# Spreading the inverted softmax denominators over the partitions by DMA instead of by a TensorE product

## What is computed

```
x = x + tanh(g_xattn[0]) * L0_xattn(layernorm(x), ctx, ctx)
x = x + tanh(g_ffn[0]) * L0_ffn(layernorm(x))
x = x + tanh(g_xattn[1]) * L1_xattn(layernorm(x), ctx, ctx)
x = x + tanh(g_ffn[1]) * L1_ffn(layernorm(x))
```

```
scores = jnp.einsum('bhqd,bhkd->bhqk', qh, kh) / jnp.sqrt(jnp.float32(d_k))
attn = jax.nn.softmax(scores, axis=-1)
context = jnp.einsum('bhqk,bhkd->bhqd', attn, vh)
return context.transpose(0, 2, 1, 3).reshape(B, S, H * dk) @ w_out + b_out
```

## Time and profile before

| | |
|---|---|
| device time, median of 3 runs | 1260.38 us (1259.9 to 1260.52) |
| span of the profiled execution | 1044.2 us |
| median less span (start and end of a launch) | 216.2 us |
| TensorE busy | 927.7 us, 89% of the span |
| VectorE busy | 624.5 us, 60% |
| ScalarE busy | 581.2 us, 56% |
| GpSimd busy | 679.4 us, 65% |
| chain that ended last | PE 57%, DVE 13%, ACT 9%, DMA 7%, issue 7%, POOL 6% |

### The profile page before, as it was taken

The page is one execution under the profiler, slowest core; times in us unless marked ns, Lnnn a source line. Parts: engine busy times, 40 slices in busy tenths (PEclk is TensorE's granted clock), DMA queues, the critical chain, the costliest instruction groups (busy, mean ns, idle before and its releaser), DMA issues.

```text
span 1044.2 us, 25012 instructions
## 1 busy us (share of the span) xinstructions
PE 927.7 (89%) x8892; PEld 777.6 (74%) x8892; DVE 624.5 (60%) x1600; ACT 581.2 (56%) x1274; POOL 679.4 (65%) x905
## 2 busy tenths in 40 slices
PE   5999988788748999999999989887998999999992
PEld 3777776566647989999999977775776767778881
DVE  5899999988964563244625759784735424533320
ACT  2888876687525446544644667554555455444540
POOL 6565556578747777377427777621686758878785
PEclk9999998899868999999999999998999999999997
DMA  9355432122145656676566663123164554574444
GB/s 367 117 177 183 153 123 100 38 67 68 52 157 161 209 176 205 201 213 188 163 193 187 195 236 103 43 71 90 17 114 49 91 68 50 81 105 54 51 54 45
DMA packets 130811, 130.87 MB, mean 125 GB/s; under 512 B 33410, under 2 KB 103426, under 8 KB 129794
## 3 DMA queue, kind: packets, MB, share of 16 engines
q1 hardware_dynamic: 100466, 91.82, 27.8%
q0 software_dynamic: 28928, 29.91, 17.5%
q10 hardware_dynamic: 1296, 7.54, 1.8%
HBM read 54.01 MB, written 49.62 MB: 99 GB/s over the span
## 4 chain that ended last, share of the span: by engine, by line
PE 57%; DVE 13%; ACT 9%; DMA 7%; issue 7%; POOL 6%; ACTq 0%; SPq 0%; POOLq 0%; DVEq 0%
PE psum L844 10%; PE psum L854 10%; PE psum L1022 9%; PE psum L1012 8%; PE psum L656 3%; ACT w_sb L1669 3%; PE psum L976 2%; POOL work L1970 2%; DVE mx L1156 2%; DVE w_sb L1162 2%; ACT work L1676 1%; PE psum L834 1%; DMA out_x<-ln_sb,dest 1%; PE psum L683 1%; DMA odd<-ln_sb,dest 1%
## 5 line engine op out<-in xcount | busy, mean ns | idle before, releaser
L1763 ACT ACTIVATE hid_sb<-psum,work 128x128 f32<-128x128 f32 (+1 forms) x424 | 145.6, 412 | 138.9 <-PE psum L844 136.6
L1970 POOL DMA_INDIRECT work<-yg,place x128 | 122.7, 959 | 73.6 <-issue 48.2
L844 PE MATMUL psum<-work 128*128 128x128 f32 (+1 forms) x848 | 150.1, 320 | 2.6 <-issue 2.3
L854 PE MATMUL psum<-w_sb,hid_sb 128*128 x1192 | 150.2, 275 | 0.0
L854 PEld LDWEIGHTS psum<-w_sb,hid_sb 128*128 128x128 f32 x1192 | 144.8, 192 | 2.1
L1012 PE MATMUL psum<-work,w_sb 128*128 128x272 f32 (+2 forms) x512 | 131.0, 397 | 5.1 <-ACT ctx_sb L1872 3.1
L2044 POOL DMA_INDIRECT out_x<-ln_sb,dest x68 | 106.2, 1562 | 45.0 <-DVE ln_sb L1586 24.8
L844 PEld LDWEIGHTS psum<-work 128*128 128x128 f32 x848 | 124.4, 192 | 11.3 <-issue 4.2
L1872 ACT ACTIVATE ctx_sb<-psum,w_sb 128x272 f32<-128x272 f32 (+2 forms) x256 | 115.8, 488 | 26.3 <-PE psum L1012 22.5
L1022 PE MATMUL psum<-ctx_sb,w_sb 128*128 128x272 f32 (+2 forms) x512 | 128.1, 392 | 0.0
L2044 POOL DMA_INDIRECT odd<-ln_sb,dest x68 | 105.5, 1552 | 32.3 <-issue 16.1
(11 more groups left out here) (241 smaller groups left out, 1762.3 us busy)
## 6 DMA issues: line engine op xcount, KB each, us to landing
work<-w_sb SPq DMA_DIRECT2D x76, 322.0 KB
work<-xg SPq DMA_DIRECT2D x73, 128.0 KB
yg<-yg_sb SPq DMA_DIRECT2D x73, 128.0 KB
xg<-yg_sb SPq DMA_DIRECT2D x24, 384.0 KB, 4.1
ctx_sb<-tok SPq DMA_DIRECT2D x8, 1088.0 KB, 6.4
ctxn<-sums_sb SPq DMA_DIRECT2D x64, 64.0 KB, 2.0
out_x<-x_sb SPq DMA_DIRECT2D x16, 256.0 KB
odd<-yg_sb SPq DMA_DIRECT2D x10, 384.0 KB, 2.9
```

The costliest lines, as they stand in the source:

```text
L844: e.matmul(banks[UP_BANKS[c]][:, 0:cols], w1g(b)[:, c * P:c * P + P], xgT_sb[:, u % 2, at:at + cols], start=True, stop=True).then_inc(s_up, 1)
L854: ins = e.matmul(banks[DOWN_BANKS[b % 2]][:, n * D:n * D + D], hid0[:, b % 2, c, n * P:n * P + P], w2_sb[:, bass.ds(number, 1), c, :].rear ...
L1763: e.activation(hid0[:, b % 2, c, 0:cols], banks[UP_BANKS[c]][:, 0:cols], ACT.Gelu, bias=w1g(b)[:, HID + c:HID + c + 1]).then_inc(s_hg, 1)
L1970: e.indirect_dma_start(dst[:, k, :], None, yg_dram[h], at).then_inc(s_get[i], 16)
```

## The change

The table, its load and TensorE's product are gone. In their place SyncE waits for the reciprocal and issues two SBUF-to-SBUF DMAs per pair into `rb_sb`, a part of `work`; each writes 128 partitions of 128 columns, reading every one of 16 rows of `den_sb` eight times. The normalisation reads `rb_sb` in place of PSUM. The denominators are brought by two DMAs of 16 partitions (in another order of rows) in place of four of 8. VectorE's reciprocal now stands ahead of stats0 in its iteration. TensorE's wait for the copied sums moves from the table's product to the output product, where it comes later. SyncE waits for the last normalisation before its loop over the expert blocks, since a weight buffer there overlays `rb_sb`.

```diff
+        rb_sb = cut(10240, dict(i=2, n=2 * P), "i n")
...
-                w.wait_ge(s_dc[i], 64 * (p // 2))
+                w.wait_ge(s_rb[i], 32 * (p // 2))
                 w.wait_ge(s_vc[i], 32 * (p // 2))
                 for a in range(2):
-                    for u in range(2):
-                        row, at = 8 * (2 * a + u), 2 * P * a + P * u
-                        e.dma_start(den_sb[row:row + 8, i, :], sums_sb[ONES:P:HEAD_ONES - ONES, i, at:at + P]).then_inc(s_dc[i], 16)
+                    e.dma_start(den_sb[16 * a:16 * a + 16, i, :], sums_sb[ONES:P:HEAD_ONES - ONES, i, 2 * P * a:2 * P * a + 2 * P]
+                                ).then_inc(s_dc[i], 16)
...
+            def spread_rden(p):
+                i = p % 2
+                w.wait_ge(s_rden, p + 1)
+                w.wait_ge(s_cn, p - 1)
+                for u in range(2):
+                    e.dma_start(rb_sb[:, i, u * P:u * P + P],
+                                den_sb[u:32:2, i, :].unsqueeze(1).to_broadcast([2 * DH, DH, P])).then_inc(s_rb[i], 16)
...
                 for _ in range(2):
                     next(filling, None)
+                spread_rden(p)
...
+            w.wait_ge(s_cn, NP)
             for b in range(NBL + 2):
...
-            def spread_rden(p):
-                w.wait_ge(s_rden, p + 1)
-                w.wait_ge(s_uc, min(p + 2, NP))
-                w.wait_ge(ld["tables"], 112)
-                for u in range(2):
-                    ins = e.matmul(banks[B_C][:, u * P:u * P + P], spread_sb[0:32, u, :], den_sb[0:32, p % 2, :], start=True, stop=True)
-                ins.then_inc(s_sp, 1)
-
             def output(p):
                 w.wait_ge(s_cn, p + 1)
+                w.wait_ge(s_uc, min(p + 2, NP))
...
-                if 0 <= p - 3 < NP:
-                    spread_rden(p - 3)
...
             def normalise(p):
                 i = p % 2
-                w.wait_ge(s_sp, p + 1)
+                w.wait_ge(s_rb[i], 32 * (p // 2 + 1))
                 w.wait_ge(s_vc[i], 32 * (p // 2 + 1))
-                e.tensor_tensor(ctxn[:, i, :], banks[B_C][:, 0:2 * P], ctxn[:, i, :], ALU.mult).then_inc(s_cn, 1)
+                e.tensor_tensor(ctxn[:, i, :], rb_sb[:, i, :], ctxn[:, i, :], ALU.mult).then_inc(s_cn, 1)
...
-                stats0(20 + 2 * p, 2)
                 if 0 <= p - 2 < NP:
                     invert(p - 2)
+                stats0(20 + 2 * p, 2)
```

More of the change, by code:

```diff
@@ L372, in build @@
             "s_v", "s_vx", "s_st0", "s_st1", "s_sc", "s_mx", "s_sub", "s_exp", "s_rden", "s_xb", "s_uc")]
-        s_pt, s_pT, s_av, s_sp, s_cn, s_o, s_x1 = [sem(n) for n in ("s_pt", "s_pT", "s_av", "s_sp", "s_cn", "s_o", "s_x1")]
-        s_dc, s_vc = [[sem(f"{n}{i}") for i in range(2)] for n in ("s_dc", "s_vc")]
+        s_pt, s_pT, s_av, s_cn, s_o, s_x1 = [sem(n) for n in ("s_pt", "s_pT", "s_av", "s_cn", "s_o", "s_x1")]
+        s_dc, s_vc, s_rb = [[sem(f"{n}{i}") for i in range(2)] for n in ("s_dc", "s_vc", "s_rb")]
         s_xT0, s_xl, s_xe, s_xlt, s_lgx, s_lg = [sem(n) for n in ("s_xT0", "s_xl", "s_xe", "s_xlt", "s_lgx", "s_lg")]
@@ L451, in sync_program @@
             for dst, src in ((small_sb, "small"), (mask_sb, "mask"), (before_sb, "before"), (block_sb, "block"), (b2T_sb, "b2T"),
-                             (rowcol_sb, "rowcol"), (spread_sb, "spread")):
+                             (rowcol_sb, "rowcol")):
                 load("tables", dst[:], t_in[src])
@@ L772, in count0 @@
                 w.wait_ge(s_ch, h + 1)
-                w.wait_ge(ld["tables"], 112)
+                w.wait_ge(ld["tables"], 96)
                 wait_bank(B_P)
@@ L1166, in invert @@
                 i = p % 2
-                w.wait_ge(s_dc[i], 64 * (p // 2 + 1))
+                w.wait_ge(s_dc[i], 32 * (p // 2 + 1))
                 e.reciprocal(den_sb[0:32, i, :], den_sb[0:32, i, :]).then_inc(s_rden, 1)
@@ L1680, in copy_sums @@
                 w.wait_ge(s_av, p + 1)
-                w.wait_ge(s_dc[i], 64 * (p // 2))
+                w.wait_ge(s_dc[i], 32 * (p // 2))
                 w.wait_ge(s_vc[i], 32 * (p // 2))
@@ L2085, in lay_out @@
     order = np.arange(D).reshape(4, 2, 2 * DH).transpose(1, 0, 2).reshape(-1)
-    spread = np.zeros((P, 2, P), np.float32)
-    for n, (pa, u, m, h) in enumerate(itertools.product(range(2), range(2), range(4), range(2))):
-        at = 64 * pa + 16 * m + DH * h
-        spread[n, u, at:at + DH] = 1.0
     w = [a["L0_xattn_w_q"], a["L0_xattn_w_k"], a["L0_xattn_w_v"], a["L0_xattn_w_out"][order], a["L1_xattn_Wq"], a["L1_xattn_Wk"],
@@ L2121, in lay_out @@
         "rowcol": f((r % NS)[:, None] + NS * np.arange(NT // NS)[None, :], r[:, None]),
-        "spread": spread,
         "before": c(np.stack([(q < k), np.ones((P, P))], 1).astype(np.float32)),
```

3 lines of the change are left out of this document (removed).

## The result

| | kernel before | changed |
|---|---|---|
| median, lowest to highest, 17 runs each, us | 1259.89, 1251.88 to 1264.28 | 1266.29, 1261.4 to 1273.89 |
| profiled execution, us | span 1044.2, no time of its own | time 1267.35, span 1265.5 |
| large maximum of iterations 3 and 17, us | 39.60, 144.49 | 39.87, 155.20 |
| one iteration between them, us | 7.49 | 8.24 |

The change makes the kernel slower, by about 0.6%: ratio 1.0057, with a 95% interval of 1.0039 to 1.0076. The forecast was 1256.0 us, 0.3% faster. Only runs in the fast state are compared; single runs, whose state is unknown, are used for their profiles alone.

A forecast was written before the change was run, and what follows sets the result against it. Attention was bound by a loop through ScalarE and TensorE, VectorE's 6.88 us next; -8.6 + 5.4 + 2.2 - 2.2 - 1.2 = -4.4 us from 1260.38 gave 1256.0 us, own range 1252 to 1258.5, overall 1250 to 1264.

The forecast's parts named there:

- What bounds the kernel: Layer 0's attention: table's product costs 1.30 us a turn; without it VectorE's 6.88 us bounds, TensorE at 6.2.
- The step that failed: Spread's landing before the normalisation: 2.65 us from the reciprocal, taken from the channels' DMA, 0.4 us to spare.
- 3.03 us of cover: Time from the reciprocal's end until VectorE alone could start the normalisation: 3.03 us.
- The -8.6 us: Gain in iterations 3 to 17: 14 turns, each 0.61 us shorter, from 7.49 to 6.88.
- The landing of 2.0 to 2.3: Sign expected in the changed profile: the spread lands 2.0 to 2.3 us after issue.
- The queue: First 19 iterations: bursts of fills, turned inputs and weights delay the spread; +5.4 us, ends 0 and about 9.
- Fills alone are over before the spread's data come: Within the queue term: iterations with only zero fills were to cause no stall.
- GpSimd's port, +2.2: Normalisation reading two SBUF tiles: +0.1 us for each of 14 plus about 8 later ones, +2.2 us.
- rival B: GpSimd holds back VectorE's normalisations, 0.4 us for each of 22: +4.2, total 1260.2 us; chance 0.15.
- Later waits and the tail, -3.4: Waits on table's and output products: -2.2 us behind iteration 17, -1.2 us at the end.
- Rival C: Attention: DMAs' latency closes a new loop, 3.85 us plus latency, break-even 3.64; 1265 us, slower; chance 0.18.
- The baseline: Profiled span of 1044.2 us against runs' median of 1260.38: 216.2 us difference, left as it was.

The follow-up runs named there:

- experiment 5: Changed kernel with normalisation, output product, residual and router's statistics one iteration later: 1041.67 us, 0.9984 of the kernel before; turn 6.86 us.
- experiment 2: Changed kernel with all 38 zero fills issued before the first pair: 1270.29 us, turn 7.59 us against 8.24 in the changed kernel.
- experiment 12: Changed kernel, fills first, spread reading 128 different partitions, beside a partner with the repeated source: turn 7.51 against 7.69 us; an earlier probe was inconclusive.
- experiment 3: Changed kernel with the spread issued right behind the sums, ahead of turned inputs, weights and fills: ratio 1.0040, turn 8.32 us.
- experiment 6: Changed kernel with all zero fills first and VectorE's reciprocal ahead of the residual: turn 7.77 us.
- experiment 10: Version of experiment 5 with a catch-up at the end: 1247.73 us, ratio 0.9936 on the first chip; 1044.50 us, ratio 1.0000 on the second.
- experiment 1: Kernel before, unedited, profiled again: 1255.41 us, ratio 0.9994, turn 7.49 us.

## Why the prediction was wrong

**What bounds the kernel: right.** The copy of the sums and the product did leave the chain, and VectorE is the next bound: 6.70 us in an undisturbed iteration of experiment 5, where I had added up 6.88. TensorE I had too low: 6.2 us a turn, where it is busy 6.65 in experiment 5.

**The step that failed** is "the landing of the second ... I take 2.65, since 2.0 is the median of 64: in a quiet queue 0.4 us to spare". The median was that of the channels' DMA, and I carried it to another DMA. The spread itself needs, from the reciprocal's end to the normalisation, 3.2 us at best of the 14 iterations (3.15 and 0.03 to the issue) and 4.39 in the mean. In the iterations of experiment 2 and of its repetition in experiment 12 whose pairs have no loads and no fills, it needs 2.9 to 4.3, in the mean 3.6 and 3.5. The Trainium skill (DMA: Bandwidth & Descriptors, Anatomy of one DMA — SWDGE (gpsimd) path) gives about 2.0 us for the fixed part of a DMA on GpSimd's path; these are issued by SyncE. The channels' DMA and the spread's quickest landings have the same 2.0, the spread's median of 3.2 beside the fills doesn't. Against the 3.03 us of cover the case without loads and fills alone turns a slack of 0.4 into a wait of 0.4 to 1.4 us in eight of ten turns, and since the wait delays the reciprocal that starts the next spread, nothing absorbs it. The -8.6 us rested on that slack; in their place stand +10.4. The landing of 2.0 to 2.3 that I forecast came as a median only in experiment 5 behind iteration 17 (2.3, from 160 to 205 us).

**The queue: right in kind, too small.** I priced it at +5.4 us and 9 at most; the waits on the spread add up to 19.2. "Fills alone are over before the spread's data come" is false: pairs 8, 9 and 11 to 13, with fills alone, waited 0.27 to 1.39. Pairs with weights and fills waited 0.78 to 1.40, where I had 0.25; those with turned inputs 2.97, 2.26 and 2.25 (pairs 2, 6 and 10), where I had 1.7, 1.7 and 0.5; and the very first pair 3.08. The issue of the spread itself takes 1.75 to 2.7 us in place of 1.28 in six of the 14, which I didn't have either; but this doesn't need the fills (up to 2.25 in experiment 2, where they are long gone), and the wait doesn't follow it: with issues of 2.19 and 1.79 the normalisation came 3.66 and 3.25 us after the start, with 1.28 up to 4.60. I costed the queue at one place, the spread, and the loop pays it each time; the other order of experiment 3 didn't dodge it.

**GpSimd's port, +2.2: it did not come, because the two never met.** All normalisations from 39 to 200 us take 0.41 to 0.43 us. That GpSimd is busy 66.63 of 115.33 us doesn't test the rule: none of them overlaps one of GpSimd's instructions on 128x128 elements or more, only some on 128x8. Where they meet, the wait is there. In the run of experiment 6:

```profile
99.43 0.73 POOL L1944 TENSOR_TENSOR x_sb<-x_sb,bias_sb 128x256 f32<-128x256 f32 x1
99.66 0.80 DVE L1173 TENSOR_TENSOR ctxn<-work,ctxn 128x256 f32<-128x256 f32 x1 [0.34 <-DMA work<-den_sb]
```

The normalisation ends 0.30 us after GpSimd's addition of the bias. Over all runs, up to 240 us, 18 normalisations start while that addition runs; they take 0.40 to 0.91 us, and every one ends 0.27 to 0.36 us after it. This agrees with the rule of the exclusive port (Trainium skill, SBUF — State Buffer, Who interferes with whom). So what I had wrong was how often the two meet, not the mechanism. In experiment 10, on the first chip, five of the first 14 normalisations take 0.49 to 0.91 us, some 1 us in all. As a cause of this result rival B is out.

**Later waits and the tail, -3.4: about -2.** From iteration 17 to 31 the changed kernel takes 150.46 us against 151.82 in experiment 1, and from there to the first expert's transposes 42.6 against 43.2; each is one profile.

**The whole time** then would be 1260.4 + 10.4 - 2 = 1269, against a measured 1266.29. The 2.7 between them are not explained. **Rival C** was this case, mechanism, loop and sum: it had 3.85 us of fixed work, a point of 3.64 us from which it decides, and 1265 us. That its time is so close to 1266.29 is in part luck: it had +2.9 for the loop and 4 for the queue where the stretch lost 10.4, and less of the loss reached the whole time than arose in the attention. I gave it 0.18, because its latency of 3.85 was the worst landing seen, when it was below the mean of what came (4.39). Its own sign for recognition, a wait on the DMA in every iteration, came true between 3 and 17.

**The baseline.** I wrote that 216.2 us between span and median were left as they are. They belong to some chips only: 176 us inside layer 0's experts, 21 between iteration 17 and these, 13 behind them. That left the size of the attention's loss untouched, but not how much of it the total shows: 0.3 to 0.6% on two chips, 1.5% on a third.

## What to carry over

Before an engine's product is replaced by DMAs, draw the loop that the DMAs would stand in: work on the loop plus latency must be below the present turn, with the latency at its mean under load, not at another DMA's median. (Experiment 6 warns that this mean can move when the loop is shortened.) If a DMA must go in, give it a whole iteration of distance first; here that turned 8.24 us a turn into 6.86 with the same transfers. And ask what gets the time that is won: at the lower level, of 9 us 7 were gone again by the experts, beside 7.4 more of waiting for GpSimd's scatters.

## What was unexpected of the hardware

- The same program ran at about 1044 or 1255 us, by chip, with 176 of some 210 us in one stage, where the profile shows waits ("issue", "remote") that it puts down to nothing in the kernel, and a mean granted clock of 0.80 in place of 0.99.
- Two SBUF-to-SBUF DMAs of 64 KB that follow each other were there 2.9 to 4.2 us after the first issue, 3.5 in the mean, in iterations without loads and fills; experiment 12 excludes the repeated source as the main reason, and the cause stays open.
- Issuing two such DMAs took up to 2.7 us in place of 1.28, up to 2.25 with no fills in the queue, and what waited for them wasn't later for it.
- A VectorE product of two SBUF tiles that started beside GpSimd's addition of two SBUF tiles ended 0.27 to 0.36 us after it, in 18 cases of 18; alone it takes 0.40 to 0.43.
- GpSimd took 20.78 us for a power over 32x128 elements.
